# Experts' gating by tanh: one more product on VectorE, the activation from another table, a new order of the merged halves

## The chip, the cores and the metric

The kernel runs on one core of a Trainium2 chip. The core's engines run side by side, each through its own list of instructions, and wait for each other by semaphores: TensorE (PE, matmuls and transposes), VectorE (DVE), ScalarE (ACT, activations from function tables), GpSimd (POOL), and SyncE (SP), which here issues every DMA. The metric is the device time of one launch in microseconds, the median of several runs.

## The reference

Eight sequences of 512 tokens with 128 features pass through four blocks, each behind a layer norm and added to its input but for the last: an attention of which only the diagonal of a column softmax is used, two layers of local attention (window 64) with a gated feed-forward, a causal attention with 16 heads, and a mixture of experts: eight experts, of which each token weighs its best two, and a shared one. The part that the change touches is the last:

```python
scores = jax.nn.softmax(x @ gate_w, axis=-1)
topk_w, topk_idx = jax.lax.top_k(scores, K)
topk_w = topk_w / (jnp.sum(topk_w, axis=-1, keepdims=True) + 1e-20)
...
for e in range(E):
    hid = jax.nn.silu(x @ w_gate[e]) * (x @ w_up[e])
    y = y + w_per_expert[:, e:e + 1] * (hid @ w_down[e])
shared = jax.nn.silu(x @ ws_gate) * (x @ ws_up) @ ws_down
return (y + shared).reshape(b, s, h)
```

## The kernel before

A sequence is worked on as four tiles of 128 tokens, or turned, with features on the partitions and 512 tokens along the free axis. All data is float32, but for some bfloat16 parts of the causal attention. The work of a sequence is cut in two halves. The *front* is `enter` (`embed`: the column attention; `project` of the first local layer) and `leave` (`attend` of layer 0, then `project` and `attend` of layer 1, with the feed-forward, and `out`, which turns the result). The *back* is the causal attention, the routing and the experts. Front and back use different PSUM banks, four each.

The program is written out for the eight sequences. `run_turns` merges, for t = 0 to 5, the back of sequence t with `leave` of t + 1 and `enter` of t + 2; a seventh merge has the back of 6 and `leave` of 7, and the back of 7 runs alone. Each half is a generator that yields ahead of each step (`yield "scores0"`), and the table `ORDER` has one string for each engine: at an F the front goes one step on, at a B the back. So the order on each engine is set by hand, the same in each merge, and every step holds its own waits (`wait_ge`). An engine goes through its list in order: a step that waits holds up what stands behind it, from whichever half.

Steps and names that the text speaks of:

- *Entry* (`embed`). PE transposes the normalised input (`tp`), projects q, k and v (`qkv`, `av`), and computes four blocks of scores (`scores0` to `scores3`, 512 columns each, one bank each). DVE takes the maximum of each block (L940), ACT the exponential with its sum (L701). DVE multiplies by the identity to keep the diagonal (L943, step `x1`), sums it (L946), scales v and adds it to the input (L952, step `diag`), takes statistics (L907, L914, `ln2`), waits for POOL's inverse root (L1241), normalises (L920, `xn2`). PE transposes again (`tp2`), ACT copies it into `h` (L707, L708), and PE projects q, k, v of the first local layer (`qk0` to `qk3`, `v01`, `v23`).
- *Rotary part* (`project`). For each of four tiles m DVE makes two products for q (step `qk`) and two for k (step `rk`), L978 and L979, and then sums of squares (step `ss`). POOL adds the products (L1266), scales k (L1277) and takes inverse roots (L1241, `ik` and at the end `iq` for the four tiles). Then PE turns q and k (`tn`, `tk`).
- *Local softmax* (`attend`). PE adds mask and similarities of tile m (`sm0` to `sm3`), DVE takes the maxima (L1011), ACT the exponentials in eight pieces (L767, steps `ex`), POOL multiplies by the inverse sums (L1297), PE turns the probabilities (`pt`), multiplies them by v (`pv`), projects (`wo`). The feed-forward follows: `mean`, `var`, `w10` to `w12`, `w1a0` to `w1a2`, `w2`, `out`.
- *Back*. `ln`, `xn`, `tp` (ACT's copy is L832), `qkv` (q and k are copied by L835 and L837), splitting into parts, packing through DRAM, row maxima (`max`, L1123), scores and exponentials (`s`, L847), `turn0` to `turn3` (L633, L1132, L1134), `otp` (PE turns `bxn`, ACT copies it by L853), `wo`, a layer norm, `tp2`, `route` (L1153 to L1193, small operations that end in `gate`).
- *Experts*. For expert e, half c of the 256 hidden features: PE computes the gate product (step `moe`*ec*`g`) and the up product (`moe`*ec*`u`), each 128x512 into one of three banks, taken in turn (n = 4e + 2c + j). ACT applies Silu to the gate product and writes `silu`, in `big` (L869). DVE multiplies the up product by it and writes `hid` (L1217, step `moe`*ec*`u`). A bank is written again when its reader is through: ACT for a gate product, DVE for an up product. In step `dn`*e* PE multiplies `hid` by the down weights, eight small matmuls into the fourth bank, and DVE adds the result times the gate into `outb` (four operations of 128x128, L1205; the shared expert, the ninth, by L1202). The steps of `dn`*e* stand behind those of expert e + 1. SP then loads the weights of a later expert.

A table load (`ACT_TABLE_LOAD`) is put in by the compiler wherever ACT needs a function that is not in the table set that is loaded.

## Time and profile before

| | us |
|---|---|
| median of 3 runs | 1952.59 |
| lowest, highest | 1950.83, 1952.88 |
| the profiled execution | 1956.37 |
| its span in the trace | 1954.3 |
| busy: PE, DVE, ACT, POOL | 1622.1, 1134.6, 985.1, 598.0 |
| mean granted clock of PE | 0.92 of full speed |

The profile is one further execution, 3.8 us above the median. The span runs from the first to the last instruction of the trace; the time of the execution is 2.1 us more. Busy times are sums over the span, and say nothing on which engine is waited for at which moment; the chain of waits does: it goes back from the last instruction, at each step to what released it. In a view of instructions the brackets hold how long the engine had been idle before the instruction and who released it. A float32 matmul shows as two records. PE's clock has two levels, 1.2 and 2.4 GHz; a granted clock of 1.00 is the upper, 0.50 the lower.

### The profile page before, as it was taken

Reading aid. Unit: us, or ns where it says so; the run is one execution under the profiler, and the core shown is the slowest. Engines: PE = TensorE matmul, PEld = TensorE weight load, DVE = VectorE, ACT = ScalarE, POOL = GpSimd, SP = SyncE. Lnnn points to the kernel's source line nnn. Section 1 sums busy time; section 2 is a strip of 40 time slices with the busy share of each in tenths; the row PEclk is TensorE's granted clock in tenths of the full one; section 3 lists DMA queues with packets and bytes.
Section 4 is the critical chain, followed back from the end, with each engine's and each line's share of the span. In section 5 each row is a group of like instructions: output and inputs, shape, how many; then the busy total and the mean of one; then the engine's idle time right before and its main releaser. Section 6 shows DMA issues by size and latency. Waiting matters only on the chain.

```text
span 1954.3 us, 30040 instructions
## 1 busy us (share of the span) xinstructions
PE 1622.1 (83%) x11568; PEld 952.2 (49%) x11632; DVE 1134.6 (58%) x2567; ACT 985.1 (50%) x2276; POOL 598.0 (31%) x394
## 2 busy tenths in 40 slices
PE   4666668898799979899789988899798988998579
PEld 2424244555445555554545555464546554455235
DVE  6342458458574576547494576557594576644514
ACT  2435243844556553854557553754548544762041
POOL 2532160605251070504333060613434061510000
PEclk8687769999899989999899998999899998999689
DMA  4010021011300132011400122001410123002301
GB/s 133 20 24 1 0 56 31 21 38 52 79 22 10 38 83 41 21 30 33 106 22 2 46 60 64 21 25 31 109 27 2 43 60 66 21 17 63 67 1 54
DMA packets 37295, 80.15 MB, mean 41 GB/s; under 512 B 6783, under 2 KB 22655, under 8 KB 33777
## 3 DMA queue, kind: packets, MB, share of 16 engines
q1 hardware_dynamic: 37152, 78.22, 15.9%
q8 instruction: 93, 1.52, 0.3%
q14 instruction: 50, 0.40, 0.1%
HBM read 54.74 MB, written 8.78 MB: 33 GB/s over the span
## 4 chain that ended last, share of the span: by engine, by line
PE 48%; DVE 18%; ACT 17%; POOL 12%; issue 4%; DMA 1%; SPq 0%; POOLq 0%; DVEq 0%; ACTq 0%
PE ps L351 42%; ACT work L767 9%; DVE cmax L1123 6%; ACT big L847 6%; PE ps L356 5%; POOL small L1241 5%; POOL work L1266 3%; POOL work L1277 2%; DVE work L978 1%; DVE work L979 1%; DVE small L1011 1%; POOL frs L1241 1%; DVE fxn L920 1%; DVE fst L907 1%; ACT ctmp L850 1%
## 5 line engine op out<-in xcount | busy, mean ns | idle before, releaser
L1266 POOL TENSOR_TENSOR work<-work 128x1024 f32<-128x1024 f32 x64 | 151.0, 2360 | 463.9 <-DVE work L979 463.4
L351 PE MATMUL ps<-bxt,mw 128*128 128x512 f32 x576 | 278.2, 606 | 7.0 <-DVE big L1217 7.0
L351 PE MATMUL ps<-maskb,identb 128*128 128x128 bf16 (+1 forms) x1120 | 227.6, 242 | 41.8 <-ACT work L767 30.7
L767 ACT ACTIVATE work<-ps,pbias,small 128x128 f32<-128x128 f32 x512 | 229.0, 525 | 45.9 <-DVE pbias L1015 45.0
L356 PE MATMUL ps<-ident,work 128*128 128x128 f32 x1056 | 175.6, 313 | 61.6 <-ACT work L767 41.0
L1123 DVE TENSOR_REDUCE cmax<-ps 128x1 f32<-128x384 f32 (+3 forms) x352 | 199.3, 631 | 24.6 <-PE ps L351 24.4
L1241 POOL TENSOR_TENSOR small<-small,consts 128x8 f32<-128x8 f32 x128 | 208.2, 1641 | 5.3 <-DVE small L988 5.3
L351 PE MATMUL ps<-wqkv,h 128*128 128x512 f32 x384 | 188.5, 624 | 22.3 <-ACT v L727 11.7
L1297 POOL TENSOR_TENSOR work<-work,prec 128x1024 f32<-128x1024 f32 x64 | 134.3, 2099 | 206.4 <-DVE prec L1006 206.4
L847 ACT ACTIVATE big<-ps 128x512 f32<-128x512 f32 x320 | 167.3, 638 | 58.3 <-PE ps L351 58.2
L869 ACT ACTIVATE big<-ps 128x512 f32<-128x512 f32 x144 | 85.2, 597 | 207.4 <-PE ps L351 206.6
L356 PEld LDWEIGHTS ps<-ident,work 128*128 128x128 f32 x1056 | 136.9, 161 | 103.2 <-ACT work L767 49.1
L351 PEld LDWEIGHTS ps<-bxt,mw 128*128 128x128 f32 x576 | 103.8, 194 | 112.4 <-issue 100.4
L351 PE MATMUL ps<-work,w 128*114 128x512 f32 (+1 forms) x288 | 148.1, 642 | 11.2 <-ACT work L807 8.7
L351 PE MATMUL ps<-pk,pq 96*128 96x512 bf16 (+3 forms) x512 | 128.0, 315 | 35.1 <-DMA pq<-scr_parts 20.4
L351 PEld LDWEIGHTS ps<-mw,big 128*128 128x128 f32 x1152 | 138.8, 192 | 34.6 <-issue 33.0
L351 PE MATMUL ps<-mw,big 128*128 128x128 f32 x1152 | 140.8, 275 | 5.2 <-DVE x L1205 5.2
L1011 DVE TENSOR_REDUCE small<-ps 128x8 f32<-128x1024 f32 x64 | 78.1, 1220 | 113.6 <-PE ps L351 113.5
L351 PEld LDWEIGHTS ps<-maskb,identb 128*128 128x128 bf16 x1152 | 113.4, 101 | 62.0 <-issue 60.8
L767 ACT ACTIVATION_READ_ACCUMULATOR work<-ps,pbias,small 128x1 f32 x512 | 138.6, 271 | 0.0
L1241 POOL TENSOR_TENSOR frs<-fmv,consts 128x4 f32<-128x4 f32 x16 | 3.2, 201 | 420.7 <-DVE fmv L914 420.7
L1217 DVE TENSOR_TENSOR big<-ps,big 128x512 f32<-128x512 f32 x144 | 97.0, 685 | 54.9 <-PE ps L351 54.4
(162 smaller groups left out, 2594.0 us busy)
## 6 DMA issues: line engine op xcount, KB each, us to landing
mw<-in_experts SPq DMA_DIRECT2D x72, 384.0 KB, 3.1
pk<-scr_parts SPq DMA_DIRECT2D x48, 192.0 KB
pq<-scr_parts SPq DMA_DIRECT2D x144, 64.0 KB
v<-v SPq DMA_DIRECT2D x16, 512.0 KB, 4.6
v<-v SPq DMA_DIRECT2D x16, 384.0 KB, 5.8
scr_parts<-big SPq DMA_DIRECT2D x8, 768.0 KB, 3.7
xin<-in_x SPq DMA_DIRECT2D x8, 256.0 KB, 3.4
out<-x SPq DMA_DIRECT2D x8, 256.0 KB, 5.4
```

What stands on the lines that cost most here:

```text
L351: return nc.tensor.matmul(o, a, b, start=start, stop=stop, skip_group_check=True)
L356: i = nc.tensor.transpose(bank[:, tt * P:(tt + 1) * P], src(tt), ident[:, :])
L767: i = nc.scalar.activation(pr[:, m, a, p, :], fb[2 * (m % 2) + a][:, p * P:(p + 1) * P], ACT.Exp, bias=pbias[:, m, k:k + 1], scale=rn[:, m ...
L847: nc.scalar.activation(big[:, n, :], bb[k % 3][:, :], ACT.Exp).then_inc(c_e.sem, 1)
L869: nc.scalar.activation(silu[e % 2][:, c, :], bb[n % 3][:, :], ACT.Silu).then_inc(m_silu.sem, 1)
L1011: nc.vector.tensor_reduce(pmax[:, m, :], fpair[m % 2].rearrange("p a (c b) -> p (a c) b", b=P), AX.X, ALU.max, negate=True).then_inc(fv.se ...
L1123: nc.vector.tensor_reduce(cmax[:, r, heads[0]:heads[-1] + 1, t], bb[k % 4][:, 0:cols * len(heads)].rearrange("p (a b) -> p a b", b=cols), ...
L1217: tt_(hid[e % 2][:, c, :], bb[n % 3][:, :], silu[e % 2][:, c, :], ALU.mult).then_inc(m_hid.sem, 1)
L1241: return nc.gpsimd.tensor_tensor(out, x, consts[:, k:k + 1].broadcast_to([x.shape[0], x.shape[1]]), op)
L1266: nc.gpsimd.tensor_tensor(qk[:, m, :], qk[:, m, :], part[m % 2], ALU.add).then_inc(l_add.sem, 1)
L1277: nc.gpsimd.tensor_tensor(k3, k3, rn[:, m, HEADS:2 * HEADS].unsqueeze(2).broadcast_to([P, HEADS, DH]), ALU.mult).then_inc(l_kn.sem, 1)
L1297: nc.gpsimd.tensor_tensor(p3, p3, prec[:, m, :].unsqueeze(2).broadcast_to([P, HEADS, P]), ALU.mult).then_inc(l_pn.sem, 1)
```

## The change

Silu(z) is z / 2 x (1 + tanh(z / 2)). ACT now computes tanh(z / 2) from the gate product. DVE adds 1 and multiplies by the gate product, which it reads from its bank: a new step `moe`*ec*`s` ahead of each `moe`*ec*`u`, 18 for each sequence. That gives twice the Silu. The factor of 2 is taken out at the end: the sum by which the gates are divided is doubled in the operation that adds 1e-20, and the shared expert's result is scaled by 0.5 in the operation that adds it. The gate product's bank is now free when DVE's new product is done (`m_gated`), not when ACT is. The strings in `ORDER` are new for PE, ACT, DVE and SP; POOL's is the same. In the changed kernel's lines everything stands one line lower up to L1200.

```diff
-    "tensor": "FBFBFFFFFFFFFFFFFBBBBFBBBBBBBBBBBBFBBFBBBFBFBBBFFBBBBFBBBBFBBBFBBFBBBFBBBBFBBBBFBBBBBBBBBBBBBBBBBFBB"
+    "tensor": "FFBBFFFFFFFFFFFFFBBBBFBBBBBBBBBBBBFBBFBFBBFBBBBFFBBBBFBBBBFBBBFBBFBBBBFBBBFBBBBFBBBBBBBBBBBBBBBBBBFF"
...
-        m_silu, m_hid, m_sum = sig("m_silu", ALL * 2), sig("m_hidden", ALL * 2), sig("m_sum", ALL)
+        m_tanh, m_gated = sig("m_tanh", ALL * 2), sig("m_gated", ALL * 2)
+        m_hid, m_sum = sig("m_hidden", ALL * 2), sig("m_sum", ALL)
...
-                                freed = m_hid if q % 2 else m_silu
+                                freed = m_hid if q % 2 else m_gated
...
-                        nc.scalar.activation(silu[e % 2][:, c, :], bb[n % 3][:, :], ACT.Silu).then_inc(m_silu.sem, 1)
+                        nc.scalar.activation(silu[e % 2][:, c, :], bb[n % 3][:, :], ACT.Tanh, scale=0.5).then_inc(m_tanh.sem, 1)
...
-                ts(rs1[:, 3, :], rs1[:, 3, :], 1e-20, None, ALU.add).then_inc(bv.sem, bv.one())
+                ts(rs1[:, 3, :], rs1[:, 3, :], 1e-20, 2.0, ALU.add, ALU.mult).then_inc(bv.sem, bv.one())
...
                     if e == EXPERTS:
-                        tt_(outb[:, :, :], bb[3][:, :].rearrange("p (a b) -> p a b", a=NT), outb[:, :, :], ALU.add).then_inc(m_sum.sem, 1)
+                        stt(out=outb[:, :, :], in0=bb[3][:, :].rearrange("p (a b) -> p a b", a=NT), scalar=0.5, in1=outb[:, :, :],
+                            op0=ALU.mult, op1=ALU.add).then_inc(m_sum.sem, 1)
                         return
...
                 for e in range(ALL):
                     for c in range(2):
+
+
+                        yield f"moe{e}{c}s"
+                        n = 4 * e + 2 * c + 1
+                        dve.wait_ge(m_tanh.sem, m_tanh.at(s, 2 * e + c + 1))
+                        stt(out=silu[e % 2][:, c, :], in0=silu[e % 2][:, c, :], scalar=1.0, in1=bb[(n - 1) % 3][:, :],
+                            op0=ALU.add, op1=ALU.mult).then_inc(m_gated.sem, 1)
                         yield f"moe{e}{c}u"
-                        n = 4 * e + 2 * c + 1
                         dve.wait_ge(m_u.sem, m_u.at(s, 2 * e + c + 1))
-                        dve.wait_ge(m_silu.sem, m_silu.at(s, 2 * e + c + 1))
+                        dve.wait_ge(m_gated.sem, m_gated.at(s, 2 * e + c + 1))
                         if e >= 2 and c == 0:
                             dve.wait_ge(m_d.sem, m_d.at(s, e - 1))
                         tt_(hid[e % 2][:, c, :], bb[n % 3][:, :], silu[e % 2][:, c, :], ALU.mult).then_inc(m_hid.sem, 1)
```

On ACT the compiled program of before has 99 table loads and the changed one has 65. None stands at the experts any more, where there were 28; at the local softmax (L767, now L768) there is one in place of seven.

*DVE, in the entry.* From the fourth maximum (before: L940; in the changed kernel L941) to the second normalisation (L920; L921), in the first merge as in the others. Before:

```order
L940 TENSOR_REDUCE small<-ps 128x1 x4
L1217 TENSOR_TENSOR big<-ps,big 128x512
L943 TENSOR_TENSOR work<-work,ident 128x512
L946 TENSOR_REDUCE small<-work 128x4
L947 RECIPROCAL small<-small 128x4
L949 TENSOR_TENSOR small<-small 128x4
L952 SCALAR_TENSOR_TENSOR x<-v,small,xin 128x128 x4
L907 BN_STATS fst<-x 128x6 x4
L912 MEMSET pause 128x1
L914 BN_AGGR fmv<-fst 128x2 x4
L1217 TENSOR_TENSOR big<-ps,big 128x512
L920 TENSOR_SCALAR fxn<-x,fmv,frs 128x128 x4
```

After, from the last two maxima on (L1225 is the product that writes `hid`, L1218 the new one, L1207 the addition of an expert):

```order
L941 TENSOR_REDUCE small<-ps 128x1 x2
L944 TENSOR_TENSOR work<-work,ident 128x512
L1225 TENSOR_TENSOR big<-ps,big 128x512
L1207 SCALAR_TENSOR_TENSOR x<-ps,gate,x 128x128 x4
L947 TENSOR_REDUCE small<-work 128x4
L948 RECIPROCAL small<-small 128x4
L950 TENSOR_TENSOR small<-small 128x4
L953 SCALAR_TENSOR_TENSOR x<-v,small,xin 128x128 x4
L1218 SCALAR_TENSOR_TENSOR big<-big,ps 128x512
L908 BN_STATS fst<-x 128x6 x4
L913 MEMSET pause 128x1
L915 BN_AGGR fmv<-fst 128x2 x4
```

Ahead of this piece the changed order has one maximum, L1225, one maximum and L1218. Behind the product with the identity now stand L1225 and the addition L1207, and behind L953 a new product; L921 follows this piece, and behind it come L1225, L1218 and L1225.

*DVE, at the first rotary products* (before L978 and L979, now L979 and L980; the first pair is q's, the second k's). Before:

```order
L978 TENSOR_TENSOR work<-ps,sinT 128x512
L979 TENSOR_TENSOR work<-ps,cosT 128x512
L978 TENSOR_TENSOR work<-ps,sinT 128x512
L979 TENSOR_TENSOR work<-ps,cosT 128x512
L986 TENSOR_REDUCE small<-work 128x16
L988 TENSOR_REDUCE small<-small 128x16
```

After:

```order
L979 TENSOR_TENSOR work<-ps,sinT 128x512
L980 TENSOR_TENSOR work<-ps,cosT 128x512
L1207 SCALAR_TENSOR_TENSOR x<-ps,gate,x 128x128 x4
L979 TENSOR_TENSOR work<-ps,sinT 128x512
L980 TENSOR_TENSOR work<-ps,cosT 128x512
L987 TENSOR_REDUCE small<-work 128x16
L989 TENSOR_REDUCE small<-small 128x16
```

The addition of an expert has moved in between q's products and k's.

*PE, at the start of the local softmax of layer 0* (`maskb` and `kt,qt` are a block of similarities, `ident,bxn` the transpose `tp` of the back, `bxt,cw` its q and k, `cw,bxt` its v). Before:

```order
L351 MATMUL ps<-mw,big 128x128 x8
L351 MATMUL ps<-maskb,identb 128x512 x2
L351 MATMUL ps<-kt,qt 64x128 x16
L356 MATMUL ps<-ident,bxn 128x128 x4
L351 MATMUL ps<-maskb,identb 128x512 x2
L351 MATMUL ps<-kt,qt 64x128 x16
L351 MATMUL ps<-bxt,cw 128x512 x2
L351 MATMUL ps<-cw,bxt 128x128 x4
L351 MATMUL ps<-maskb,identb 128x512 x2
```

After:

```order
L352 MATMUL ps<-mw,big 128x128 x8
L352 MATMUL ps<-maskb,identb 128x512 x2
L352 MATMUL ps<-kt,qt 64x128 x16
L352 MATMUL ps<-maskb,identb 128x512 x2
L352 MATMUL ps<-kt,qt 64x128 x16
L357 MATMUL ps<-ident,bxn 128x128 x4
L352 MATMUL ps<-bxt,cw 128x512 x2
L352 MATMUL ps<-cw,bxt 128x128 x4
L352 MATMUL ps<-maskb,identb 128x512 x2
```

The second block of similarities stands ahead of the back's transpose, and the back's q and k follow the transpose directly.

Further moves in a merge: on ACT the copy of `otp` (L853) stands ahead of the last four exponentials of the local softmax of layer 1, where it stood behind them, and on PE `wo` of the back ahead of `pt1`; PE's `tp2` of the back stands ahead of `pv2` and `pv3`, and the route and the first gate product ahead of the front's `wo`; expert 4's second gate product stands behind `out` and no longer ahead of it. On SP the load of the next input stands one step earlier.

## Rows read from the trace of the kernel before

**Rows 1.** The page: busy time and share of the span by engine; the chain by engine.
```profile
PE 1622.1 (83%) x11568; PEld 952.2 (49%) x11632; DVE 1134.6 (58%) x2567; ACT 985.1 (50%) x2276; POOL 598.0 (31%) x394
...
PE 48%; DVE 18%; ACT 17%; POOL 12%; issue 4%; DMA 1%; SPq 0%; POOLq 0%; DVEq 0%; ACTq 0%
```

**Rows 2.** Groups of ACT: shapes xcount | busy us, mean ns | idle before.
```profile
L847 ACT ACTIVATE big<-ps 128x512 f32<-128x512 f32 x320 | 167.3, 638 | 58.3 <-PE ps L351 58.2
...
L869 ACT ACT_TABLE_LOAD x28 | 35.9, 1283 | 0.5
```

**Rows 3.** Groups of DVE, same view.
```profile
L1217 DVE TENSOR_TENSOR big<-ps,big 128x512 f32<-128x512 f32 x144 | 97.0, 685 | 54.9 <-PE ps L351 54.4
...
L1050 DVE SCALAR_TENSOR_TENSOR work<-ps,b,work 114x512 f32<-114x512 f32 x48 | 35.2, 745 | 52.6 <-ACT work L813 37.4 <-PE ps L351 14.6
```

**Rows 4.** The chain of waits, 1060 to 1160 us: start, length, what.
```profile
1064.11 20.34 PE ps L351 x76
...
1087.14 13.31 PE ps L351 x42
...
1128.97 2.37 POOL work L1266
...
1150.52 6.39 POOL small L1241 x4
```

**Rows 5.** Timeline of DVE, 1109 to 1128 us: start, length, what [idle before].
```profile
1114.17 0.69 DVE L940 TENSOR_REDUCE small<-ps 128x1 f32<-128x512 f32 x1 [0.17 <-PE ps L351]
1114.78 0.68 DVE L1217 TENSOR_TENSOR big<-ps,big 128x512 f32<-128x512 f32 x1
1115.71 0.69 DVE L943 TENSOR_TENSOR work<-work,ident 128x512 f32<-128x512 f32 x1 [0.25 <-ACT work L701]
...
1119.82 0.66 DVE L1217 TENSOR_TENSOR big<-ps,big 128x512 f32<-128x512 f32 x1
1121.30 1.12 DVE L920 TENSOR_SCALAR fxn<-x,fmv,frs 128x128 f32<-128x128 f32 x4 [0.82 <-POOL frs L1241]
...
1126.41 0.69 DVE L978 TENSOR_TENSOR work<-ps,sinT 128x512 f32<-128x512 f32 x1 [2.96 <-PE ps L351]
```

**Rows 6.** Timeline of POOL, 1120 to 1150 us.
```profile
1134.19 2.36 POOL L1266 TENSOR_TENSOR work<-work 128x1024 f32<-128x1024 f32 x1 [1.25 <-DVE work L979]
...
1139.43 2.37 POOL L1266 TENSOR_TENSOR work<-work 128x1024 f32<-128x1024 f32 x1 [0.27 <-DVE work L979]
```

**Rows 7.** Timeline of PE, 1152 to 1170 us.
```profile
1159.36 0.66 PE L356 MATMUL ps<-ident,bxn 128*128 128x128 f32 x4 [3.21 <-DVE bxn L920]
...
1160.38 1.85 PE L351 MATMUL ps<-kt,qt 64*64 64x128 f32 x32
1162.16 2.87 PE L351 MATMUL ps<-bxt,cw 128*128 128x512 f32 x4
```

**Rows 8.** Busy time by stretch: PE, PEld, DVE, ACT, POOL, granted clock, DMA share.
```profile
1160.00:1164.00 4.00, 4.00 (x37) 2.29 (x35) 1.39 (x2) 2.36 (x9) 0.00 (x0) 0.57 0.03 10
```

**Rows 9.** Timeline of PE, 1050 to 1064 us.
```profile
1053.48 0.66 PE L356 MATMUL ps<-ident,bxn 128*128 128x128 f32 x4 [0.72 <-DVE bxn L1134]
1055.19 1.09 PE L356 MATMUL ps<-ident,work 128*128 128x128 f32 x8 [1.05 <-ACT work L767]
```

**Rows 10.** Timeline of ACT, 1050 to 1090 us.
```profile
1054.78 0.84 ACT L853 COPY bxt<-ps 128x512 f32<-128x512 f32 x1
...
1087.11 1.28 ACT L869 ACT_TABLE_LOAD   x1
```

**Rows 11.** Timeline of PE, 896 to 908 us: the same turn as at 1122 us.
```profile
901.15 1.11 PE L356 MATMUL ps<-ident,fxn 128*128 128x128 f32 x4 [0.81 <-DVE fxn L920]
```

**Rows 12.** Timeline of PE, 1905 to 1916 us.
```profile
1910.70 3.60 PE L351 MATMUL ps<-bxt,mw 128*128 128x512 f32 x8
```

**Rows 13.** The chain of waits, its last piece.
```profile
1897.58 49.84 PE ps L351 x208
```

14 lines of the change are left out of this document (7 added, 7 removed).

## The prediction

> **What bounds the kernel now.** I read the page first. TensorE (PE) is busy for 83% of the span and makes up 48% of the chain that ended last, but VectorE (DVE), ScalarE (ACT) and GpSimd (POOL) hold 18, 17 and 12% of it [rows 1]: no engine bounds the whole, and each stage of a period has its own. The kernel works in seven merged periods, 221 to 225 us apart. The chain in order of time says who leads where [rows 4]. From 1064 us the front's last products (out projection, feed-forward) and experts 0 to 4 of the back are one unbroken run of PE, 20.34 and then 13.31 us. Then comes the entry of the next sequence: column attention, a layer norm, the first projection, a chain that goes from DVE to ACT to PE and back. From 1128.97 it is POOL's: rotary sums, inverse roots, norms, up to the four roots that start at 1150.52 and take 6.39 us. After that the local softmax runs on ACT. The last sequence alone ends in 49.84 us of PE [rows 13].
>
> The profiled execution took 1956.37 us, 3.8 above the median of the three runs (1952.59). I add up against the first and carry the difference to the second.
>
> **The table loads.** The program of before has 99 loads of a function table on ACT, the changed one 65: the 28 at the experts [rows 2] go, and six of the seven behind them, at the local softmax. 34 x 1.283 = 43.6 us of ACT's work go. What of it lies on the path? The load at 1087.11 stands between the front's normalised rows and its Gelu, right inside the 13.31 us in which PE runs without a gap [rows 4, 10]; the others of the expert stage stand beside the same two runs; the one for the local softmax ends before POOL's roots are done. I take 0. The bound on the side of a gain: the two loads behind the normalised rows stood in the way in all seven periods, 14 x 1.283 = 18 us. They can't cost anything by going, so 0 is the other bound.
>
> In the Trainium skill, "ScalarE: Activation LUTs", section "What ACT_TABLE_LOAD costs", a switch of sets is said to cost 1.28 us and a drain of about 1.38 more, 2.66 in all; by it 90 us of ACT would go instead of 43.6. The load's own 1283 ns agrees with our rows; all 28 loads together have 0.5 us of idle time before them [rows 2], and I don't count a drain. Beside PE's unbroken run either figure gives 0.
>
> **The products on DVE.** 144 new products of 128x512 read PSUM and SBUF. The nearest row is the same kind of instruction on 114x512, 745 ns, against 685 for the plain product [rows 3]; in a row one starts 0.61 after the other for a 0.69 instruction [rows 5], so I price one at 0.67 in a row: 96 us on DVE, 12 per sequence. The scale moves onto the routing sum and the shared expert's sum, no instruction more. Of the 18 products of a period, ten fall before the entry of the next sequence, beside PE's unbroken run, where DVE waits for PE anyway: 0. Eight fall into the entry and POOL's stretch, where DVE is on the path or nearly so.
>
> *Entry.* Before, the four maxima of the column scores are followed by one expert product, and the product with the identity starts at 1115.71, when the fourth exponential is out [rows 5]. Now two expert steps stand among the maxima: a reduction, the hidden product, a reduction, the new product, two reductions. The fourth reduction ends about 0.5 us later. Then, behind the product with the identity, come a hidden product (0.60) and the addition of an expert (1.05) before the sum of the diagonal: 1.65, less 0.1 that the other product no longer holds. Then one new product stands before the statistics: 0.67. Before, the expert product at 1119.82 lay in POOL's 1.3 us of roots and cost nothing. Sum: 0.5 + 1.55 + 0.67 = 2.7 us later at the second normalisation (1121.30 before). The ends: 1.0, if only the addition is exposed, and 3.5.
>
> *What shifts the entry itself.* ACT now copies the transposed column-attention output ahead of the last four exponentials and must wait for it: PE's transpose of that output starts at 1053.48 and takes 0.66 [rows 9], so the copy runs from 1054.1 to 1054.6 at the soonest and four exponentials of 0.44 each follow to 1056.6; before, the exponentials came first, the copy started at 1054.78 [rows 10] and PE's next turns, which wait for the last exponential, at 1055.19 [rows 9]. They start 1.4 later. PE makes up 0.9 of it by having the out projection done meanwhile, and then has a transpose of 0.7 more in the row: +1.25 at the end of the probabilities' product. Against this, the transpose is no longer behind it (0.66), one expert matmul (four take 3.60 with a pipeline's tail, so 0.86 each [rows 12]) stands behind the entry's start instead of before it, and one now stands before the entry's projections (0.25 not hidden). Sum: 1.25 - 0.66 - 0.86 + 0.25 = 0.0, within 1 either way. I take -0.1.
>
> *POOL's stretch.* The projection's first rotary products start when PE has them, at 1126.41 before, 2.6 later now. Between those of q and of k there now stands an expert addition (1.05), so POOL's first sum is 3.6 late. POOL had 1.25 us of waiting before its second sum [rows 6] and takes most of it back: +2.3. Then PE does two expert matmuls before the values' projection where it did one (0.86 late), ACT and DVE hand this on, and the third sum is 2.9 late; it had 0.27 of waiting. From there POOL's own work sets the pace (two sums start 5.24 us apart [rows 6]). The new products that fall there add 0.67 or 1.3 to a step of DVE's; I take it that DVE still ends its step inside POOL's 5.2. So POOL ends 2.9 us late, in the six periods in which a sequence enters. The ends: 0.5 (POOL's slack takes all but the addition) and 4.5.
>
> **Edits of the order elsewhere.** *Local softmax of the next layer.* PE waits 3.21 us for the back's normalised input at 1159.36, then transposes it, does the second block of similarities and only then the back's q and k [rows 7]. Now the second block goes first, into the wait. Between transpose (ended at 1160.02) and q lies ACT's copy, 0.7 with its handing over, so q starts at 1160.7 and not at 1162.16, 1.4 earlier; ACT's exponentials stand behind k's copy. The clock is low there (0.57 granted, the level of 1.2 GHz for most of it [rows 8]), so k, at 1.43 each, ends 1.3 earlier. Gain 1.3 in seven periods; the ends are 0.5 (the third block's maximum then comes last) and 2.8 (the clock stays at 2.4 GHz). *Exponentials of the back*: their 320 fills wait 58.3 us for PE in all [rows 2], most of it ahead of a group; the new order feeds two fills per period earlier, for which I take 0.3, between 0 and 1. The maxima's steps are the same work in the same run: 0. *Last sequence*: the first product waits behind the routing and the last sum takes 0.06 more: +0.2; elsewhere the bank is free in time, since an activation (0.60) and a product (0.75) fit into the two matmuls (1.72) that PE has before it.
>
> **Sum.** 6 x 2.9 - 7 x 1.3 - 7 x 0.3 + 0.5 (the shift of 1.25 less 0.66 in the last merged period, in which nothing enters) + 0.2 = 17.4 - 9.1 - 2.1 + 0.7 = +6.9. 1956.37 + 6.9 = 1963.3; against the median 1952.59 + 6.9 = **1959.5 us**.
>
> **Rivals.** *The products are hidden* (faster). If the entry's insertions land in waits of DVE for PE and POOL's slack swallows the addition, 6 x 0.5 is left, and the gains of the local softmax stand: 3.0 - 9.1 - 2.1 + 0.7 = -7.5, 1945. It decides as soon as the entry costs less than about 1.9 per period. For it: DVE is idle 2.96 us at 1126.41 [rows 5]. Against: the insertions stand ahead of that point, and what DVE waits for there is its own result, by way of PE. *In between*, an entry of 1.5 to 2.2: 1949 to 1955. *The clock* (slower). In the period at 901.15 the entry's transpose already takes 1.11 instead of 0.66 us, the 1.2 GHz level [rows 11], after gaps on PE. The change adds 2 to 3 us of gap there. If the other three periods' transpose and projections (about 3.4 us) fall to that level too, and the others stay there longer, 6 x 2 = 12 come on top: 1971. *The table loads are on the path* (faster): up to 18 and half of the gain above, 1952.6 - 18 - 7 = 1927; against it stands PE's unbroken run [rows 4].
>
> The Trainium skill, "ScalarE: Activation LUTs", section "Table sets: the hidden batching unit", gives the rule to batch calls by set; by it this change is right and the last rival is the one to back. The number of loads does fall as the rule says; that they are not waited for is what rows 4 say.
>
> **How the numbers follow.** The forecast: 0.50, with a range of its own of 1954 to 1967. Products hidden: 0.22, 1941 to 1949. In between: 0.10. Clock: 0.15, 1966 to 1979. Loads: 0.03, 1915 to 1941. The range from 1942 to 1974 leaves out the loads, half of the clock's case and the edges. A measurement of this kernel tells about 0.2% (3.9 us) from no change, so "same" is 1948.7 to 1956.5: 0.10 of the in-between case, 0.12 from the forecast's lower part. Faster: 0.22 + 0.03 = 0.25. Slower: 0.38 + 0.15 = 0.53.
>
> **What would show it.** Right: 65 loads on ACT and its busy time down by some 40 us; DVE's up by about 100; in the entry, 2 to 3 us more from the fourth maximum to the second normalisation; POOL's first rotary sum without 1.25 of wait behind it; q and k of the back directly behind their transpose, a good microsecond earlier. Wrong: if POOL's four roots start as soon after the run of PE as before; if the softmax's exponentials don't come earlier; or if PE's two runs now have gaps that wait for the new product on DVE.

## The result, and the profile after

| | before | after |
|---|---|---|
| median, us | 1952.74 (8 runs) | 1959.15 (8 runs) |
| lowest, highest | 1941.22, 1953.78 | 1957.52, 1960.69 |
| ratio, 95% interval | | 1.0040 (1.0024 to 1.0055) |
| span of the profiled execution | 1954.3 | 1958.8 |
| granted clock of PE, mean | 0.920 | 0.929 |

The changed kernel is 6.4 us slower, 0.4 below the forecast of 1959.5. The sum came out; its terms did not all. Two executions further on took far longer than the others of their kernel (one of the kernel before 2435.25 us, one of the changed kernel with three matmuls added 5492.04); the medians contain them, the ratios leave them out.

The page of the changed kernel, the lines that answer to [rows 1]:

```profile
PE 1617.0 (83%) x11568; PEld 939.8 (48%) x11632; DVE 1226.1 (63%) x2711; ACT 942.1 (48%) x2242; POOL 597.0 (30%) x394
...
PE 44%; DVE 22%; ACT 15%; POOL 12%; issue 5%; DMA 1%; SPq 0%; POOLq 0%; DVEq 0%; ACTq 0%
```

ACT is busy for 43 us less and DVE for 91.5 more, as forecast (40 and 100). The groups of ACT and DVE (shapes, count, busy us, mean ns, idle before), for [rows 2, 3]:

```profile
L848 ACT ACTIVATE big<-ps 128x512 f32<-128x512 f32 x320 | 164.7, 640 | 60.2 <-PE ps L352 60.1
...
L870 ACT ACTIVATE big<-ps 128x512 f32<-128x512 f32 x144 | 85.8, 596 | 198.3 <-PE ps L352 198.3
...
L1225 DVE TENSOR_TENSOR big<-ps,big 128x512 f32<-128x512 f32 x144 | 99.0, 687 | 11.6 <-PE ps L352 2.8
L1218 DVE SCALAR_TENSOR_TENSOR big<-big,ps 128x512 f32<-128x512 f32 x144 | 98.3, 682 | 14.5 <-ACT big L870 13.2
```

The new product takes 682 ns, as the plain one does. The 28 table loads of L869 have no successor. The exponentials of the back still wait 60.2 us for PE (58.3 before), so the 0.3 us per period that the forecast gave the new order there did not come.

To see where the time went I cut each of the merged periods at the same instructions of both traces and took the mean of the first six:

| stretch of a period, us | before | after | difference | forecast |
|---|---|---|---|---|
| back's first transpose to first root of layer 1 | 66.29 | 63.89 | -2.40 | -1.6 |
| from there to the transpose of `otp` | 48.75 | 49.64 | +0.89 | 0 |
| from there to the entry's first transpose | 52.68 | 51.43 | -1.25 | -0.35 |
| entry's first transpose to its second | 17.09 | 19.68 | +2.59 | +2.95 |
| from there to the first root behind q | 9.32 | 11.04 | +1.72 | |
| from there to the four roots | 19.18 | 18.75 | -0.43 | together +0.3 |
| whole period (with 8.88 before the transpose) | 222.19 | 223.32 | +1.13 | +1.3 |

The forecast's figures are its terms laid on these stretches (2.7 and the 0.25 ahead of the projections in the fourth row, the rest of the shift in the third, both terms of the softmax in the first). The last two stretches come to +1.29 where it had +0.3.

**Between the roots and `otp`** the new order feeds the back's fills earlier, and this is what they cost. Timelines of PE in the fourth merged period, before and after: the first similarities of layer 1. The four roots started at 1028.13 before and at 1026.09 after, so the block starts 4.18 us behind them before and 4.99 after; two fills of the back and their matmuls stand ahead of it now. Of these 0.8, 0.74 are still there at `otp`.

```profile
1032.31 1.10 PE L351 MATMUL ps<-kt,qt 64*64 64x128 f32 x32
```
```profile
1031.08 1.10 PE L352 MATMUL ps<-kt,qt 64*64 64x128 f32 x32
```

**The entry**, for [rows 5]: timeline of DVE in the fifth merged period of the changed kernel.

```profile
1334.54 0.68 DVE L1218 SCALAR_TENSOR_TENSOR big<-big,ps 128x512 f32<-128x512 f32 x1
1335.13 1.28 DVE L941 TENSOR_REDUCE small<-ps 128x1 f32<-128x512 f32 x2
1337.33 0.69 DVE L944 TENSOR_TENSOR work<-work,ident 128x512 f32<-128x512 f32 x1 [0.92 <-ACT work L702]
1337.94 0.68 DVE L1225 TENSOR_TENSOR big<-ps,big 128x512 f32<-128x512 f32 x1
1338.54 1.12 DVE L1207 SCALAR_TENSOR_TENSOR x<-ps,gate,x 128x128 f32<-128x128 f32 x4
...
1341.62 0.68 DVE L1218 SCALAR_TENSOR_TENSOR big<-big,ps 128x512 f32<-128x512 f32 x1
...
1344.90 1.11 DVE L921 TENSOR_SCALAR fxn<-x,fmv,frs 128x128 f32<-128x128 f32 x4 [1.40 <-POOL frs L1249]
```

The hidden product and the addition stand bare behind the product with the identity, and a new product ahead of the statistics. From the end of the fourth maximum (1336.41) to the second normalisation it is 8.49 us; before, 1114.86 to 1121.30, 6.44. The wait of DVE for POOL's root is bare now as well (1.40, where it was 0.82).

**POOL**, for [rows 6], timeline of the same period. Between the first root (1357.44) and the second sum (1359.07) there is no wait left; the slack of 1.25 is gone, and 1.14 stand before the third sum.

```profile
1355.13 2.36 POOL L1274 TENSOR_TENSOR work<-work 128x1024 f32<-128x1024 f32 x1 [10.27 <-DVE work L980]
1357.44 1.66 POOL L1249 TENSOR_TENSOR small<-small,consts 128x8 f32<-128x8 f32 x1
1359.07 2.36 POOL L1274 TENSOR_TENSOR work<-work 128x1024 f32<-128x1024 f32 x1
...
1365.16 2.36 POOL L1274 TENSOR_TENSOR work<-work 128x1024 f32<-128x1024 f32 x1 [1.14 <-DVE work L980]
```

**The clock.** Two timelines of PE in the changed kernel, around the entry's second transpose, in the second merged period and in the third:

```profile
677.07 0.66 PE L357 MATMUL ps<-ident,fxn 128*128 128x128 f32 x4 [0.81 <-DVE fxn L921]
678.99 3.70 PE L352 MATMUL ps<-wqkv,h 128*128 128x512 f32 x8 [1.26 <-ACT h L709]
...
898.59 0.66 PE L357 MATMUL ps<-ident,fxn 128*128 128x128 f32 x4 [0.80 <-DVE fxn L921]
900.50 5.39 PE L352 MATMUL ps<-wqkv,h 128*128 128x512 f32 x8 [1.26 <-ACT h L709]
```

The same eight records take 3.70 us in the one and 5.39 in the other. In the second period the granted clock is 1.00 throughout and the first root comes 9.86 us after the transpose; in the third it falls to 0.50, the level of 1.2 GHz, and the root comes after 11.54. It falls there in five of the six periods (before: in three of six, at 9.84 against 8.82 us). So the term of 1.29 in the table is 0.60 from the order (28.60 from the second transpose to the four roots without a fall, against 28.00) and about 0.7 from the clock.

The local softmax has lower clock levels too. The answer to [rows 7, 8], timeline of PE and busy time by stretch (busy of PE, PEld, DVE, ACT, POOL; the granted clock is the third number from the end) in the fourth merged period of the changed kernel:

```profile
937.77 0.86 PE L357 MATMUL ps<-ident,bxn 128*128 128x128 f32 x4 [1.91 <-DVE bxn L921]
939.31 3.78 PE L352 MATMUL ps<-bxt,cw 128*128 128x512 f32 x4 [0.67 <-ACT bxt L833]
942.88 1.92 PE L352 MATMUL ps<-cw,bxt 128*128 128x128 f32 x8
...
939.00:943.00 4.00, 3.69 (x5) 1.63 (x6) 0.12 (x1) 2.63 (x10) 0.00 (x0) 0.50 0.00 0
```

The back's q and k do start right behind the copy, as forecast, 0.7 us after the transpose and not 2.1. But the same two matmuls take 1.98 us where the clock is up (at 1146.95 in the run with the similarities block alone, below) and 3.78 here. Over the 30 us that hold this stage, the granted clock was 0.77 before and 0.83 after (fifth period of each, before first):

```profile
1157.00:1187.00 30.00, 21.10 (x278) 16.18 (x280) 14.28 (x25) 20.79 (x75) 10.52 (x6) 0.77 0.44 103
```
```profile
1160.00:1190.00 30.00, 20.00 (x249) 14.75 (x247) 13.59 (x25) 20.76 (x75) 10.22 (x5) 0.83 0.42 99
```

I added up the time at the lower level from the granted clock of consecutive stretches of 2 us, over merged periods 2 to 6: 21.2 us per period before, 15.7 after. Whether the gain in the softmax was the place of the similarities block or the clock, the two traces can't say. The experiments do.

### The profile page after: what moved, and what is told of

Same layout as the page of the kernel before. It is cut to its first block, busy times and chain, and to the rows that moved or that the text cites. A ratio compares the mean times of both kernels' runs of the same rounds, so it can differ in the third digit from the quotient of the medians.

```text
span 1958.8 us, 30158 instructions
## 1 busy us (share of the span) xinstructions
PE 1617.0 (83%) x11568; PEld 939.8 (48%) x11632; DVE 1226.1 (63%) x2711; ACT 942.1 (48%) x2242; POOL 597.0 (30%) x394
## 4 chain that ended last, share of the span: by engine, by line
PE 44%; DVE 22%; ACT 15%; POOL 12%; issue 5%; DMA 1%; SPq 0%; POOLq 0%; DVEq 0%; ACTq 0%
PE ps L352 40%; ACT work L768 6%; DVE cmax L1124 6%; ACT big L848 6%; POOL small L1249 5%; PE ps L357 5%; POOL work L1274 2%; POOL work L1285 2%; DVE small L1012 2%; DVE work L980 1%; DVE work L979 1%; POOL frs L1249 1%; POOL brs L1249 1%; DVE bxn L921 1%; DVE fxn L921 1%
## 5 line engine op out<-in xcount | busy, mean ns | idle before, releaser
L352 PE MATMUL ps<-bxt,mw 128*128 128x512 f32 x576 | 280.1, 604 | 12.1 <-DVE big L1218 11.8
L768 ACT ACTIVATE work<-ps,pbias,small 128x128 f32<-128x128 f32 x512 | 229.0, 514 | 51.9 <-DVE pbias L1016 51.0
L352 PE MATMUL ps<-wqkv,h 128*128 128x512 f32 x384 | 197.3, 646 | 35.3 <-ACT v L728 18.3
L357 PE MATMUL ps<-ident,work 128*128 128x128 f32 x1056 | 168.0, 306 | 67.0 <-ACT work L768 43.4
L1124 DVE TENSOR_REDUCE cmax<-ps 128x1 f32<-128x384 f32 (+3 forms) x352 | 200.5, 633 | 22.3 <-PE ps L352 21.5
L848 ACT ACTIVATE big<-ps 128x512 f32<-128x512 f32 x320 | 164.7, 640 | 60.2 <-PE ps L352 60.1
L357 PEld LDWEIGHTS ps<-ident,work 128*128 128x128 f32 x1056 | 132.3, 157 | 101.7 <-ACT work L768 50.0
L352 PE MATMUL ps<-work,w 128*114 128x512 f32 (+1 forms) x288 | 142.7, 626 | 10.4 <-ACT work L808 8.7
L352 PEld LDWEIGHTS ps<-wqkv,h 128*128 128x128 f32 x384 | 72.3, 203 | 128.1 <-issue 71.4
L768 ACT ACTIVATION_READ_ACCUMULATOR work<-ps,pbias,small 128x1 f32 x512 | 133.7, 261 | 0.0
```

Source lines behind the costliest of these rows:

```text
L352: return nc.tensor.matmul(o, a, b, start=start, stop=stop, skip_group_check=True)
L357: i = nc.tensor.transpose(bank[:, tt * P:(tt + 1) * P], src(tt), ident[:, :])
L768: i = nc.scalar.activation(pr[:, m, a, p, :], fb[2 * (m % 2) + a][:, p * P:(p + 1) * P], ACT.Exp, bias=pbias[:, m, k:k + 1], scale=rn[:, m ...
L848: nc.scalar.activation(big[:, n, :], bb[k % 3][:, :], ACT.Exp).then_inc(c_e.sem, 1)
L1124: nc.vector.tensor_reduce(cmax[:, r, heads[0]:heads[-1] + 1, t], bb[k % 4][:, 0:cols * len(heads)].rearrange("p (a b) -> p a b", b=cols), ...
```

## The experiments

Each run is stated as its median and its ratio to the kernel before on the same chip. The first four ran beside a kernel before of 1949.98 us, the next four beside 1952.11, the last four beside 1950.05. Differences of medians across these groups carry the up to 2.8 us by which the kernel before differs from group to group. By the ratios, the 9.6, 16 and 18.6 us that stand below are 7.4, 13 and 17.

### The new order with the old activation

Against the changed kernel, cut where dots stand; the strings in `ORDER` stay, and the two factors that take out the 2 go with the product.

```diff
-                        nc.scalar.activation(silu[e % 2][:, c, :], bb[n % 3][:, :], ACT.Tanh, scale=0.5).then_inc(m_tanh.sem, 1)
+                        nc.scalar.activation(silu[e % 2][:, c, :], bb[n % 3][:, :], ACT.Silu).then_inc(m_silu.sem, 1)
...
                         yield f"moe{e}{c}s"
...
-                        dve.wait_ge(m_tanh.sem, m_tanh.at(s, 2 * e + c + 1))
-                        stt(out=silu[e % 2][:, c, :], in0=silu[e % 2][:, c, :], scalar=1.0, in1=bb[(n - 1) % 3][:, :],
-                            op0=ALU.add, op1=ALU.mult).then_inc(m_gated.sem, 1)
```

> The changed order with the gating of before: Silu on ACT, no new product on DVE, 34 table loads back. The step of the new product is empty. My theory (the loads lie beside other work, the products cost in the entry): the entry from its first to its second transpose loses the exposed product (0.67) and some of the delay of the fourth maximum (0.5), so some 7 us less than the changed kernel, 1952 (1949 to 1955). Rival, the loads are on the path: slower than the changed kernel, 1962 or more, up to 1977.

Measured: 1949.55 us, ratio 1.0002 (0.9988 to 1.0015). The change less its products and plus its 34 table loads is the kernel before, to within what can be measured; so the products, with all that they push, cost 9.6 us (7.4 by the ratios): they take 98.3 us of DVE's time, and a tenth of that or less reaches the kernel's. In the entry the stretch from transpose to transpose is 18.60: 1.5 of its 2.6 us come from the new order (the addition and the hidden product behind the identity's), 1.1 from the new product.

### The products in the old order

The code of the changed kernel with the strings of the kernel before on PE, ACT and SP. DVE's string is that of before with a B put in for each new step `s`; its second line, before and in this run:

```diff
-        "FFBFBFBBBBBBBBBFBBBFBBBFFBBFFFBFFBFBFBFFFFBFFFBFBFFFBBFFBFFFFFFBBBFFBBFBFFB",
+        "FFBFBFBBBBBBBBBBFBBBBBFBBBBBFFBBBBFFFBFFBBFBBFBFFFFBBFFFBBFBBFFFBBBFFBFFFFFFBBBBBFFBBBBFBFFB",
```

> The changed gating (tanh, new product, 34 loads fewer) in the order of before; each new product stands directly ahead of the product that writes hid, but that of expert 6's first half, which has to stand before the first rotary products. My theory: 1.2 to 2 us per period more on DVE in the entry and among the rotary steps, none of the gain at the local softmax: 1952.7 + 10 = 1963 (1959 to 1968). Rival, the loads are on the path: faster than before, 1935 to 1950.

Measured: 2012.84 us, ratio 1.0326 (1.0295 to 1.0357), far outside what I expected. One group of PE, the experts' first matmuls (idle time before them at the end of the line), in this kernel, then in the changed one, then in that of the new order with Silu:

```profile
L352 PE MATMUL ps<-bxt,mw 128*128 128x512 f32 x576 | 288.4, 622 | 65.0 <-DVE big L1218 65.0
```
```profile
L352 PE MATMUL ps<-bxt,mw 128*128 128x512 f32 x576 | 280.1, 604 | 12.1 <-DVE big L1218 11.8
```
```profile
L351 PE MATMUL ps<-bxt,mw 128*128 128x512 f32 x576 | 274.8, 598 | 3.2 <-ACT big L869 3.2
```

PE waits 65.0 us for the new product, which frees the gate's bank; with the new order 12.1. The difference, 52.9, is close to that of the medians, 53.7. I had priced the ten products of a period beside PE's long runs at nothing, and that holds only for the new order: it lays each `s` step apart from its `u`. In the old order the stretch from `otp` to the entry alone is 5.2 us longer than in the kernel before (57.87 against 52.68).

### The similarities block alone

```diff
-    "tensor": "FBFBFFFFFFFFFFFFFBBBBFBB...
+    "tensor": "FFBBFFFFFFFFFFFFFBBBBFBB...
```

> Before, with one move in PE's order: the second block of similarities ahead of the back's transpose. My theory: 1.3 us (by the prediction) to 2.4 us (by the two traces) less in each of seven periods: 1936 to 1944. Rival, the gain seen between the transposes and the rotary sums comes from the other moves or from the clock: 1950 to 1953.

Measured: 1931.37 us, ratio 0.9913 (0.9885 to 0.9941): 18.6 us off the kernel before by one exchange of two steps on PE, twice the 9.1 of the forecast and more than I expected here. Over the same 30 us as above the granted clock is 0.89:

```profile
1143.00:1173.00 30.00, 20.22 (x280) 15.32 (x280) 14.40 (x25) 20.57 (x75) 10.78 (x7) 0.89 0.48 110
```

The time at the lower level is 10.9 us per period and was 21.2. That speaks for the clock as the cause, and doesn't prove it.

### The table loads alone

Silu is replaced by the hyperbolic tangent in the kernel before, and nothing else, so another function is computed.

```diff
-                        nc.scalar.activation(silu[e % 2][:, c, :], bb[n % 3][:, :], ACT.Silu)
+                        nc.scalar.activation(silu[e % 2][:, c, :], bb[n % 3][:, :], ACT.Tanh)
```

> Before, with Tanh in place of Silu on ACT and nothing else: the gating is another function, but every instruction stays where it is and only the 34 table loads are gone. My theory: within 1 us of before, 1952 to 1954. Rival, the loads are on the path: 2 to 18 us less, 1935 to 1951.

Measured: 1952.4 us, ratio 1.0018 (1.0004 to 1.0031). ACT's busy time falls by 44.7 us, and its wait for PE at this line grows from 207.4 to 234.6:

```profile
PE 1628.9 (83%) x11632; PEld 952.2 (49%) x11632; DVE 1136.3 (58%) x2567; ACT 940.4 (48%) x2242; POOL 598.4 (31%) x394
...
L869 ACT ACTIVATE big<-ps 128x512 f32<-128x512 f32 x144 | 85.0, 595 | 234.6 <-PE ps L351 234.6
```

Nothing of the 34 loads was on the path. The Trainium skill, "ScalarE: Activation LUTs", section "What ACT_TABLE_LOAD costs", adds a drain of 1.38 us to each switch; by its figures, as an estimate, 34 x 2.66 = 90 us would have come off if drain and load were exposed, and none did. No drain shows in the trace of the kernel before either: its 28 loads at this line have 0.5 us of idle time before them in all.

### The expert addition moved away from q and k

DVE in the merged order, F the entering sequence, B the expert stage (the addition is `dn5`):

```diff
 F qk0.0
-B dn5
 F rk0.0
 F ss0.0
 F qk1.0
 F rk1.0
+B dn5
 F ss1.0
```

> The changed kernel with one step moved on VectorE: the expert addition (dn5), which stands between the product of q and that of k with their roots on POOL's side (behind qk0, ahead of rk0), is put behind rk1.0. Nothing else differs. Theory (the addition sits on the path there for its full 1.04 us, by the stretch from second transpose to first root of 9.86 against 8.82 us): minus 1.04 us in each of six periods, so about 6 us less than the changed kernel, some 1953 us; and where the granted clock no longer falls there the five periods of 11.1 to 11.5 us go to 9.8, which would give 1947. Rival (TensorE's own work sets the pace in that stretch and the addition is hidden): within 2 us of 1959.

Measured: 1961.69 us, ratio 1.0056 (1.0038 to 1.0075). No gain; my theory fell. DVE and POOL around it, third merged period:

```profile
905.55 0.69 DVE L979 TENSOR_TENSOR work<-ps,sinT 128x512 f32<-128x512 f32 x1 [2.92 <-PE ps L352]
...
910.72 0.69 DVE L979 TENSOR_TENSOR work<-ps,sinT 128x512 f32<-128x512 f32 x1 [1.33 <-PE ps L352]
...
913.12 1.11 DVE L1207 SCALAR_TENSOR_TENSOR x<-ps,gate,x 128x128 f32<-128x128 f32 x4
```
```profile
908.12 2.35 POOL L1274 TENSOR_TENSOR work<-work 128x1024 f32<-128x1024 f32 x1 [8.62 <-DVE work L980]
910.43 1.64 POOL L1249 TENSOR_TENSOR small<-small,consts 128x8 f32<-128x8 f32 x1
913.28 2.36 POOL L1274 TENSOR_TENSOR work<-work 128x1024 f32<-128x1024 f32 x1 [1.21 <-DVE work L980]
```

The first root does come earlier (mean 10.20 us after the transpose, 11.04 in the changed kernel). But DVE then waits 1.33 us for PE's second tile, POOL 1.21 for DVE, and the addition stands in front of the next step. To the four roots it is 30.08 us against 29.79. The price of an operation there is not that of its place between q and k; from the second tile on the stretch is paced by another chain.

### One product into POOL's root

```diff
-B moe60s
 F ln2
+B moe60s
 F xn2
```

> The changed kernel with one step moved on VectorE: the new product that stands directly ahead of the entry's second normalisation statistics (moe60s, 0.67 us) is put behind these statistics, into the time in which VectorE waits for POOL's root. Theory (everything from the first transpose to the second in the entry is one chain through VectorE, so an operation ahead of the statistics counts in full): minus 0.67 us in each of six periods, 4 us in all, about 1955 us. Rival (the second transpose waits for TensorE's expert matmul and not for the statistics): within 1.5 us of 1959.

Measured: 1952.82 us, ratio 1.0011 (0.9993 to 1.0029), so 6 us less than the changed kernel, somewhat more than the theory's 4, and not by its mechanism. Timeline of PE ahead of the second transpose, third merged period:

```profile
899.23 2.08 PE L352 MATMUL ps<-bxt,mw 128*128 128x512 f32 x2 [3.16 <-DVE big L1218]
901.10 2.44 PE L352 MATMUL ps<-mw,big 128*128 128x128 f32 x16
903.37 0.60 PE L357 MATMUL ps<-ident,fxn 128*128 128x128 f32 x4
```

PE now waits for the product instead, and its expert matmuls stand ahead of the transpose: 20.00 us from transpose to transpose where the clock stays up, not the theory's 19.0; the rival had the right wait. In this execution three of six periods have no fall of the clock in the entry; in the other three it falls before the transpose (21.2 to 21.5 us) and is over, or nearly, when q and k are projected, so the first root comes at 9.8 to 10.2 us in place of 11.0. But this execution took 1960.09 us, 7.3 above the median and the slowest of ten, and its periods (223.60 us in the mean) are no shorter than those of the changed kernel (223.32). So the trace doesn't hold the 6 us. What speaks for the clock is the granted clock of the runs: 0.933 to 0.938 in the other nine (1951.57 to 1954.96 us), 0.928 in this one, 0.929 to 0.933 in the eight of the changed kernel. Where in the period it is gained is not shown.

### The entry cleared

```diff
 F scores3
+B moe51s
 F ln2
+B moe51u
 F xn2
+B dn4, moe60s, moe60u, moe61s
 F ss0.0
+B moe61u
 F rk1.0
+B dn5
```

Each + marks the new place of steps that stood elsewhere; PE's string changes with it in three places, which are left out here.

> The changed kernel with all new VectorE work and the two expert additions taken out of the entry's chain: products 51s behind the maxima, 60s, 60u, 61s behind the second normalisation, 61u behind the first statistics of q and k, the expert addition dn5 behind rk1; on TensorE the two expert matmuls that need them go behind the second transpose and behind the values. All 144 products are still made. Theory (a product costs only where it stands ahead of the chain from transpose to transpose, 19.7 us against 17.1 us before, and of q's and k's product): minus 2.6 and minus 1.04 us in each of six periods, and minus 1.3 where the clock stays up: 15 to 30 us less, 1930 to 1944 us. Rival (VectorE has no room in this stretch, so the same work comes out of the rotary stretch instead: it grows from 29.8 us by what the entry loses): within 5 us of 1959.

Measured: 1943.32 us, ratio 0.9972 (0.9945 to 0.9998), 16 us less than the changed kernel with all 144 products made. From transpose to transpose it is 17.21 again; 0.9 of the 2.5 comes back behind it (30.71 to the four roots, 29.79 in the changed kernel), part of it as clock: the first root comes after 9.38 us in three periods and after 11.1 to 12.0 in the others. The profile is of an execution of 1950.98 us; the ten runs fall into six of 1939.65 to 1943.51 at a granted clock of 0.929 to 0.936 and four of 1950.67 to 1952.83 at 0.923 to 0.927, so the 16 us are those of the six. Theory and rival each hold for a part.

### The similarities block put back

```diff
-    "tensor": "FFBBFFFFFFFFFFFFFBBBBFBB...
+    "tensor": "FBFBFFFFFFFFFFFFFBBBBFBB...
```

> The changed kernel with one thing undone: in the local softmax TensorE again makes the second similarities block behind the back's transpose and not ahead of it. Theory (that move is worth what the stretches before and after show, 66.3 against 63.9 us from transpose to first root, in seven places): plus 2.4 times 7, about 1976 us. My own size of it in the forecast (1.3 us each, from the idle time ahead of the softmax alone) would give 1968 us. Rival (the stretch got shorter by something else that the change moved, such as the products' places): within 3 us of 1959.

Measured: 1963.36 us, ratio 1.0061 (1.0040 to 1.0082). The same exchange of two steps that was worth 18.6 us in the kernel before is worth about 4 in the changed one, hardly more than the scatter, where it takes the stretch behind the transpose from 64.91 to 63.89 us. A price of the place itself, the same in both kernels, is then some 4 us, and 14 or so of the 18.6 must come from elsewhere.

### The clock kept up

Four kernels with matmuls whose result nobody reads, meant for time in which PE waits: identity times a weight block, 128x512, into a bank that is free. But for one wait on ACT ahead of the first of them no other instruction changes, and the front's steps for the first sequence get none.

```diff
+            def fill(bank, n):
+                for _ in range(n):
+                    mm(bank, ident[:, :], wqkv[:, 0, 0:T])
...
                 yield "tp2"
+                if not is_first(s):
+                    pe.wait_ge(a_e.sem, a_e.at(s, 4))
+                    fill(fb[3], 1)
                 pe.wait_ge(f_xn.sem, f_xn.at(s, 2))
                 turn_tiles(fb[0], lambda tt: fxn[:, tt, :]).then_inc(f_tp.sem, 1)
+                if not is_first(s):
+                    fill(fb[3], 2)
```

The first has these three fills alone:

> The changed kernel with three idle-time matmuls added per sequence on TensorE around the entry's second transpose: one product of the identity with a weight block (128x512, f32, about 0.45 us at full clock) ahead of the wait for the normalised input, two behind the transposes, into a bank that nobody reads. They compute nothing that is used; everything else is as it was. Theory (in five of six periods the granted clock is 0.5 for about 3.4 us just as q and k are projected, because TensorE stood idle before, and this costs 1.2 to 1.7 us on the way to the first root): the clock stays at 1.0, the stretch from second transpose to first root is 9.86 us in all six periods, minus 1.2 x 6 = 7 us, about 1952 us. Rival (the fall is set by something other than TensorE's idle time there): no change, or up to 2 us more for the added work.

Measured: 1953.47 us, ratio 1.0018 (1.0005 to 1.0031). Timeline of PE and the stretch of 11 us from the transpose on, fifth merged period:

```profile
1341.69 1.02 PE L352 MATMUL ps<-wqkv,ident 128*128 128x512 f32 x2
1342.66 0.65 PE L357 MATMUL ps<-ident,fxn 128*128 128x128 f32 x4
1343.15 1.88 PE L352 MATMUL ps<-wqkv,ident 128*128 128x512 f32 x4
1344.87 3.60 PE L352 MATMUL ps<-wqkv,h 128*128 128x512 f32 x8
...
1342.00:1353.00 11.00, 9.74 (x26) 4.18 (x25) 8.57 (x19) 3.92 (x7) 2.61 (x2) 1.00 0.12 36
```

The granted clock is 1.00, the projection takes 3.60 in every period, and the first root comes after 10.04 in all six (9.86 plus 0.18 for the fills). That is 5.7 us by the medians, 4.3 by the ratios: the clock's price in the entry. (One fill is two records and takes about 0.9 us, not the 0.45 that I expected.)

The other three add three fills ahead of the back's first transpose (`fill(bb[1], 3)`) and, in layer 0, three ahead of `sm3` and of `pt0` and four ahead of `pt1` (into `bb[0]`). The kernel before with them, and one fill ahead of `tp2`:

> The kernel before with the matmuls that nobody reads of e10, the similarities in their old order. Theory (most of the 20 us that the new place of the similarities block saved was the granted clock: a stretch of 14 us at 0.5 shrank to 7): with the clock kept up by other means the kernel before gains 20 to 30 us, 1922 to 1932 us, and the place of the block is worth 1 us or less in each of seven places, so that e10 is at most 7 us under it. Rival (the place itself is what counts): e12 gains 10 us at most, 1942 us or more, and lies 20 us or more over e10.

Measured: 1931.16 us, ratio 0.9892 (0.9865 to 0.9918). The same 30 us:

```profile
1141.00:1171.00 30.00, 28.79 (x307) 17.93 (x307) 13.48 (x25) 20.79 (x75) 10.16 (x5) 1.00 0.46 106
```

The same with the similarities block ahead of the transpose:

> The kernel before with the second similarities block ahead of the back's transpose (as in e3) and with matmuls of identity by weights that nobody reads added in TensorE's idle time: one ahead of the entry's second transpose, three ahead of the back's first transpose, and in the local softmax of the first layer three ahead of the fourth similarities block, three ahead of the first turning of probabilities and four ahead of the second. Theory (the two stretches at a granted clock of 0.5 in each period, 7 us in the local softmax and 3.4 us in the entry, are on the path): minus 1.0 us per period in the entry and minus 2 to 3 in the softmax, about 20 us less than e3, 1911 us. Rival (in the softmax ScalarE's exponentials set the pace and TensorE's clock there costs nothing): minus 5 us, 1926.

Measured: 1930.26 us, ratio 0.9889 (0.9864 to 0.9913). The two are the same, and the same as the exchange without fills (1931.37). From the four roots to the first root of layer 1 it is 71.58 us in the one and 71.76 in the other, in periods in which the clock stays up. That looks as if the place were worth nothing at full clock. It isn't quite so: with the exchange, the three fills no longer fit into the wait. Timeline of PE, fifth merged period, without the exchange and with it:

```profile
1139.64 2.84 PE L351 MATMUL ps<-wqkv,ident 128*128 128x512 f32 x6
1142.93 0.66 PE L356 MATMUL ps<-ident,bxn 128*128 128x128 f32 x4 [0.45 <-DVE bxn L934]
```
```profile
1141.86 2.84 PE L351 MATMUL ps<-wqkv,ident 128*128 128x512 f32 x6
1144.54 0.60 PE L356 MATMUL ps<-ident,bxn 128*128 128x128 f32 x4
```

The transpose no longer waits for its input but for the fills, and comes 9.85 us behind the four roots, where it was 8.89. In the first merged period, where it has more room, the stretch is 71.57 without the exchange and 70.85 with it. And in the run with the exchange alone the clock is up until 13.7 us behind the transpose: from the first exponential to the ninth, the first behind the copies of q and k, it is 5.22 us there, 5.90 in the kernel before with fills and 7.3 to 7.5 in five of the six periods of the kernel before. So at full clock the place is worth 0.7 us, about 5 in seven periods (an estimate from these rows), which fits the 4 us above. The other 12 to 14 of the 18.6 are clock.

My expectation of 1911 for both together fell: what the fills keep up in the softmax, the exchange had already saved, as far as it was on the path, and in two periods of three a fall comes later, 48 to 55 us behind the roots. (This trace is of an execution of 1938.12 us, the slowest of four; the others took 1927.55 to 1932.69.)

The changed kernel with the fills of both kinds:

> The changed kernel with both sets of matmuls that nobody reads: those of e9 around the entry's second transpose and those of e10 ahead of the back's first transpose and in the first layer's local softmax. Theory: as e9 in the entry (minus 7), and in the softmax the stretches at a granted clock of 0.5 (some 3 and 7 us in each period) go, minus 2 to 3 us in seven places: 1930 to 1938 us. Since the clock no longer differs, its distance to e10 is what the change's schedule and products cost by themselves. Rival: as for e10, 1952.

Measured: 1948.44 us, ratio 0.9989 (0.9978 to 1.0001).

| per period, merged periods 2 to 6 | before | after | before, filled | after, filled |
|---|---|---|---|---|
| us at the lower level of the clock | 21.2 | 15.7 | 2.7 | 4.1 |
| median of the kernel, us | 1949.98 to 1952.74 | 1959.15 | 1931.16 | 1948.44 |

With fills in both, the changed kernel is 17.3 us slower; without, 6.4. Not all of the 17.3 is the change's. Periods without any fall take 220.1 us in the changed kernel and 217.3 in the kernel before, 2.8 apart. The fills themselves make up 0.9 of that: 0.7 ahead of the back's transpose (9.59 us behind the roots, 8.88 without fills), where they don't fit into the wait since the changed kernel has the exchange, and 0.18 in the entry, where it has two fills more. So the change costs about 1.9 us per period at full clock, 11 in the six periods in which a sequence enters (an estimate from these rows), where it costs 6 x 1.13 = 6.8 as it runs. The clock, which falls less under the new order, gives back the difference, some 5 us (4.5 in these six periods).

## Why the prediction was right

- **Table loads, 0:** right, shown by the run without them. (The periods of the kernel before are 220.3 to 225.3 us long, and not 221 to 225.)
- **Products:** 0.67 a piece, right (682 ns, one 0.60 behind the other). That ten of 18 per period are hidden is right, and it is the order's doing: in the old one they cost 53 us more.
- **Entry, +2.7, with 0.25 ahead of the projections:** measured +2.59. Its parts: 1.51 from the order alone (forecast 0.5 + 1.55), 1.08 from the products (forecast 0.67 + 0.25).
- **Shift of the entry, -0.1, which is -0.35 without the 0.25 counted above:** from `otp` to the entry's transpose -1.25, of which 0.8 is a fall of the clock behind the `otp` transposes that before has in half of the periods (11.5 us from these transposes to the back's next ones and not 9.93) and the changed kernel never. Without it it is -0.45, as forecast. The late turning of the probabilities came as forecast, too: it starts 3.10 us behind `otp` and not 1.71. (The copy takes 0.84 by its own row and not 0.5; with four exponentials of 0.44 that is 1056.7, next to the forecast's 1056.6.)
- **POOL's stretch:** the slack of 1.25 went, as forecast. The term was too small by 1.0 per period, +1.29 in place of +0.3. 0.7 of that is the clock, which the forecast kept as a rival at 0.15 with "the other three periods fall to that level too". Two of those three do, which makes five of six; it costs about 4 us over six periods, where the rival had 12.
- **Local softmax, -1.3 in seven periods:** here the reasoning fell short, though the direction was right. -2.4 was measured for it and the exponentials together. The forecast has q start 1.4 earlier at an unchanged low clock and that hand on in full. At full clock 0.7 is handed on; put back in the changed kernel, the block is worth 4 us in all and not 9.1. The larger part of what shortens the stretch in the kernel before is where the clock falls and for how long. The row that gave 0.57 for the clock there [rows 8] was read as a surrounding, and it was most of the cause.
- **Exponentials of the back, -0.3:** the sign was wrong. The step priced what the back gains by two fills that come earlier and not what the front loses: its similarities start 0.8 us later (read in the fourth period), and the stretch to `otp` is 0.9 longer in all six. The run with the new order and Silu has it too (26.08 us from the roots to `otp`, 25.35 before), the one with the exchange alone not (25.36).
- **Last sequence and last merge, +0.7:** from the `otp` of the seventh merge to the end of the span it is 236.3 us before and 236.8 after, +0.5.

So 6.9 was the sum of an entry sized well (2 us too dear), a rotary stretch and a stretch of the back's fills 6 and 5 us too cheap, and a softmax and a shift whose gains were 5 to 6 us too small each, the shift's by the clock and the softmax's for the larger part. The errors cancelled: that the forecast agrees to 0.4 us is luck and not a measure of the reasoning. The sign is safer: the entry's price holds with or without the fills (19.68 us without, and with them in five of six periods), and with the clock kept up the change is slower by more.

## What to carry to other kernels

Look at the granted clock by stretch before pricing a move on PE: a reordering of two steps was worth 18.6 us where its place alone gives about 5, because it changed where the clock falls, and the same gain could be had by matmuls that nobody reads. The two didn't add up. Such matmuls have to fit into the wait that they fill: three of them cost up to 1 us per period where they didn't, and a comparison of two filled kernels must leave that out. Compare the profiled execution with the median, too: two of the profiles here are 7 to 8 us above it, and a third is of an execution with a lower granted clock than most. A new operation on an engine that is half idle is free only if the order sets it apart from the operation that waits for it; the same 144 products cost 10 us in one order and 63 in another. The 34 loads taken off an engine that waits for PE gave nothing back.

## What the runs showed of the hardware

The clock fell in stages in which PE never stood still for more than 3.2 us at a time and was busy for 21.10 of 30 us (granted clock 0.77). It fell in some periods and not in others with the same instructions in the same order, in the entry of the kernel before in three of six; a kernel's runs can spread with it, as those of the one with the cleared entry do (six at 0.929 to 0.936, four at 0.923 to 0.927 and some 10 us longer).

At the lower level a chain of float32 matmuls takes 3.78 us in place of 1.98, so nearly twice as long, but most of that was hidden: over merged periods 2 to 6 the fills took 18.4 us per period of low clock from the kernel before, and its period became 4.0 us shorter, 222.56 to 218.55. The Trainium skill, "TensorE: Matmul & The Clock Gate", section "HAM oscillation — how this bites in real kernels", counts half of the throttled time as lost; that would be 9.2 here, and the traces show about a fifth. What a fall costs depends on who is waited for. 6.8 us at the lower level in the softmax, from 13.7 to 20.5 us behind the back's transpose, cost 0.8 (58.89 us from the ninth exponential to the first root with the exchange alone, 58.13 in the kernel before with fills); PE has waits of 2.0, 2.2 and 2.6 us for ACT shortly before and in it. The same 6.8 us in the feed-forward cost 2.9 (61.03 in the fourth period of the latter). Of 3.4 us behind the `otp` transposes 1.6 are lost (53.46 against 51.89), in the entry 1.0 (9.84 against 8.82).

With the clock kept up in the softmax it could fall more often later, in the feed-forward, 48 to 55 us behind the roots: 4.1 us per period at the lower level there with exchange and fills against 0 with the exchange alone, 3.4 against 1.4 in the changed kernel. In the kernel before it was 1.4 with fills and 2.0 without.
